# One router pass per group, gates made later, token sums on GpSimd: a float32 Strassen kernel on one core

## The chip, the cores and the metric

The kernel runs on one core of a Trainium2 chip. The metric is the time of one execution on the device in microseconds (us), lower is better. TensorE (PE in the rows) multiplies, VectorE (DVE), ScalarE (ACT) and GpSimd (POOL) work on tiles, and transfers are issued by SyncE (SP), ScalarE and GpSimd.

## The reference

`x` is 8 sequences of 256 tokens with 1024 features. Each sequence picks one of eight 1024x1024 matrices; its result goes through a base matrix and a mixture of eight low-rank adapters of rank 16 with a top-2 router.

```python
c = einsum('bsi,boi->bso', x, cond_weight[ids])          # xc below
probs = softmax(c @ W_router.T)                          # 8 experts
topk_p, topk_i = top_k(probs, 2); topk_p /= sum(topk_p)
combine = sum(one_hot(topk_i, 8) * topk_p[..., None], axis=1)
h = einsum('nd,erd->ner', c, A_stack) * combine[..., None]
lora = einsum('ner,eor->no', h, B_stack) * 2.0
out = x + c @ W_base.T + b_base + lora
```

## The kernel before

Two sequences are a pair (512 tokens), two pairs are a group; there are two groups, g = 0 and 1, and each goes through two products.

**First product.** For sequence s and output tile t (8 of 128 rows), `cond(s, t)` runs 8 wide matmuls (L827) and 8 narrow ones (L831) into one of four banks `bank_x`. ScalarE copies the low half out of the bank (L521), VectorE adds (L705) into `xp`, ScalarE rounds `xp` to the high part of `xc_hl` (L526), VectorE subtracts for the low part (L710). Every float32 operand of a product is such a pair of high and low parts: a "split" is a ScalarE cast (`hi`, L492) and then a VectorE subtraction (`lo`, L553), 128x1024 each. After each pair of sequences TensorE runs `router(p)` (L871: true float32, 32 of the 128 columns of the array for each of four token blocks, so 32 matmuls, which the trace shows as 64 records) and `lora_down(p)` (24 matmuls, the low-rank product, into bank_y1).

**Second product.** The base matrix is multiplied by a form of Strassen's scheme (Winograd's) in seven products, in the order P1, P2, P5, P6, P7, P4, P3. Each is 4 output tiles m of 12 matmuls (L812 to L814); P2, P7, P4 and P3 add 3 matmuls of `lora_up` to each tile, from the gated low-rank result `h_hl` (pair 0 of the group for P2 and P4, pair 1 for P7 and P3). Before products P5, P6, P7 and P4 stand "T" sums of tokens (two 128x1024 subtractions in `xp`), before P5, P6, P7 and P3 "S" sums of weights (two of 128x1024 in `raw`); all are on VectorE (L557), and each sum is then split. Results leave the banks by `first_pass` (L596; t1 after P1, t2 after P6) and `last_pass` (L604; C11 after P2). TensorE waits for the passes before it writes a bank again: P5 tile m for C11 m, P7 tile m for t2 m.

**Gates.** `make_gate(p)` on VectorE transposes the logits and goes through 16 small operations, each waiting for the one before, with one exponential on ScalarE. GpSimd then issues 4 small DMAs that spread the gate over rows (`gate_to_rows`, L440), VectorE multiplies (`gate_h`, L618), ScalarE rounds (`h_high`) and VectorE subtracts (`h_low`, L622). The gate of a group's first pair is made in the first product, after its second sequence; that of the second pair in the "window" between the products. GpSimd also issues the residual loads (L425) and the stores (L431). Every engine works through its own list in program order.

Of the kernel before, what the change touches and what calls it, by code (L numbers as in the profile page):

```python
# [144 lines left out]
def sum_order():  # L145
    order = [("bd", 0, 0)]
    for g in range(GROUPS):
        for kind, j in (("T", P5), ("S", P5), ("T", P6), ("S", P6), ("T", P7), ("S", P7), ("T", P4), ("S", P3)):
            order += [(kind, g, (j, 0)), (kind, g, (j, 1))]
    return order  # L150


SUM = {key: n + 1 for n, key in enumerate(sum_order())}


# [52 lines left out]
def build(nc, x, ids, w_cond, w_base, w_router, lora_a, lora_b, bias, consts, out):  # L208
    with ExitStack() as ctx:
# [27 lines left out]
        logit_sb = sb("logit_sb", [P, NQ, NR])  # L237
        logit = logit_sb[:, :, 0:EXPERTS]
# [14 lines left out]
        ps_logit, ps_h, ps_warm = bank_y[0], bank_y[1], bank_y[3]  # L253
# [12 lines left out]
        summed = sem("summed")  # L266
        cond_done = sem("cond_done")
# [4 lines left out]
        router_done = sem("router_done")  # L272
        gate_step = sem("gate_step")
# [19 lines left out]
        GATE_STEPS = 14  # L293
# [119 lines left out]
        def _(pool):  # L413
# [28 lines left out]

            for g in range(GROUPS):
# [25 lines left out]
        def _(act):  # L469
            def hi(key):  # L470
                kind, i, j = key
                if key in SUM:
                    act.wait_ge(summed, SUM[key])
                elif kind == "S":
# [6 lines left out]

                if kind == "S" and j[0] >= P5:
                    act.wait_ge(product_done, made(i, j[0] - 2, 2 * j[1] + 1))
# [14 lines left out]
            def exp_and_h(p):  # L498
                act.wait_ge(gate_step, p * GATE_STEPS + 3)
                nc.scalar.activation(expd[:], shifted[:], ACT.Exp).then_inc(exp_done, 1)  # L500
                act.wait_ge(h_done, p + 1)
                if p:
                    act.wait_ge(h_split, p)
                nc.scalar.copy(h_sb[:], ps_h[:]).then_inc(h_copied, 1)
# [10 lines left out]
            for g in range(GROUPS):  # L515
                stages = base_splits(g)
                for s in range(GSEQS * g, GSEQS * (g + 1)):
                    for t in range(KT):
# [11 lines left out]
                        if s % GSEQS == 2 and t == 2:  # L530
                            h_high(2 * g)
                    if s % GSEQS == 1:
                        exp_and_h(2 * g)

                for key in stages["window"][:2]:
                    hi(key)
                for key in stages["window"][2:]:
                    hi(key)
                exp_and_h(2 * g + 1)
                for key in stages[P1]:  # L540
                    hi(key)
                h_high(2 * g + 1)
                for j in (P2, P5, P6, P7, P4, P3):
# [4 lines left out]
        def _(dve):  # L548
# [9 lines left out]

            def t_sum(j):
                for h in range(2):  # L560
                    x11, x21 = half(xp[:, 0, 0:HT], h), half(xp[:, 0, HT:KT], h)
                    x12, x22 = half(xp[:, 1, 0:HT], h), half(xp[:, 1, HT:KT], h)
                    if j == P5:
                        total(x11, x12, x11, ALU.subtract)
                    elif j == P6:
                        total(x11, x22, x11, ALU.subtract)
                    elif j == P7:
                        total(x12, x22, x12, ALU.subtract)
                    else:
                        total(x11, x21, x11, ALU.subtract)  # L570
# [44 lines left out]
            def gate_h(p):  # L615
                dve.wait_ge(gate_in, 16 * CG * (p + 1))
                dve.wait_ge(h_copied, p + 1)
                nc.vector.tensor_tensor(h_sb[:], h_sb[:], gate_rows[:], ALU.mult).then_inc(h_gated, 1)  # L618
# [5 lines left out]

            def make_gate(p):
# [379 lines left out]
```

## Time and profile before

| | |
|---|---|
| median of 3 runs | 395.6 us (395.04 to 395.6) |
| the profiled execution, its own time | 395.35 us |
| its span in the profile | 393.6 us |
| TensorE busy | 389.0 us, 99% |
| VectorE busy | 302.3 us, 77% |
| ScalarE busy | 184.1 us, 47% |
| GpSimd busy | 49.9 us, 13% |
| granted TensorE clock | full in every slice |

The span is what the trace covers; 1.75 us of the execution's time lie around it. Busy shares are means over stages: in the second product VectorE is busy far more than 77%.

### The profile page before, as it was taken

To read this page: it belongs to the slowest core of one execution; us is meant where nothing else is said; L and a number is where in the kernel's file an instruction comes from. 1 tells how busy PE (TensorE), PEld (TensorE's weight loads), DVE (VectorE), ACT (ScalarE), POOL (GpSimd) and SP (SyncE) were. 2 spreads that over 40 slices of the span, in tenths; PEclk is the share of its full clock that TensorE was granted. 3 is DMA by queue.
4 is the path that set the end of the run, shared out by engine and by line. 5 is a ranking of instruction groups with operands and counts; after the bars stand their busy time and mean duration, and the time that the engine had idled before them with its cause. 6 is when DMAs were issued, how large, how long until landed. Compare 5 with 4: busy or idle time off the path is not lost.

```text
span 393.6 us, 5707 instructions
## 1 busy us (share of the span) xinstructions
PE 389.0 (99%) x2185; PEld 332.2 (84%) x2185; DVE 302.3 (77%) x431; ACT 184.1 (47%) x281; POOL 49.9 (13%) x84
## 2 busy tenths in 40 slices
PE   8999999999999999999999999999999999999997
PEld 7888888888888888888888888888888888888886
DVE  4797866779699999974548786778867999998322
ACT  5877734748642444332147666357656224441000
POOL 0101103110002130021130000260000202201110
PEclk9999999999999999999999999999999999999999
DMA  7998875868433146586668667499083302552222
GB/s 249 398 361 285 298 261 113 293 220 304 153 107 27 56 144 185 175 263 220 206 216 290 229 216 263 115 246 393 23 264 110 77 6 81 181 168 80 82 80 80
DMA packets 21979, 73.95 MB, mean 188 GB/s; under 512 B 3344, under 2 KB 3600, under 8 KB 21952
## 3 DMA queue, kind: packets, MB, share of 16 engines
q1 hardware_dynamic: 15984, 55.58, 41.1%
q0 software_dynamic: 5680, 16.96, 14.6%
q10 hardware_dynamic: 288, 1.05, 0.7%
q8 instruction: 17, 0.28, 0.3%
q14 instruction: 10, 0.08, 0.1%
HBM read 64.13 MB, written 8.39 MB: 184 GB/s over the span
## 4 chain that ended last, share of the span: by engine, by line
PE 98%; DMA 1%; ACT 0%; DVE 0%; ACTq 0%; issue 0%
PE bank_x L827 30%; PE bank_x L831 15%; PE bank_y L812 9%; PE bank_y L813 8%; PE bank_y L814 8%; PE bank_x L814 8%; PE bank_x L813 8%; PE bank_x L812 8%; PE bank_y L871 2%; DMA raw<-x 1%; ACT x_hl L510 0%; DVE out_sb L612 0%; ACTq L348 0%; ACT wc_hl L510 0%
## 5 line engine op out<-in xcount | busy, mean ns | idle before, releaser
L827 PE MATMUL bank_x<-x_hl,wc_hl 128*128 128x512 f32 x512 | 128.7, 393 | 0.6 <-ACT wc_hl L510 0.6
L553 DVE TENSOR_TENSOR wc_hl<-raw,wc_hl 128x1024 fp32r<-128x1024 f32 x90 | 108.5, 1221 | 18.6 <-ACT wc_hl L492 18.4
L492 ACT CAST wc_hl<-raw 128x1024 fp32r<-128x1024 f32 x90 | 93.6, 1051 | 56.3 <-DVE raw L557 22.8
L827 PEld LDWEIGHTS bank_x<-x_hl,wc_hl 128*128 128x128 f32 x512 | 92.1, 189 | 17.7 <-ACT wc_hl L510 1.3
L831 PEld LDWEIGHTS bank_x<-x_hl,wc_hl 128*128 128x128 f32 x512 | 70.0, 190 | 5.1
L831 PE MATMUL bank_x<-x_hl,wc_hl 128*128 128x256 f32 x512 | 71.5, 282 | 0.0
L521 ACT COPY xc_low<-bank_x 128x256 f32<-128x256 f32 x64 | 23.7, 370 | 35.2 <-PE bank_x L831 35.2
L705 DVE TENSOR_TENSOR xp<-bank_x,xc_low 128x256 f32<-128x256 f32 x64 | 27.0, 422 | 15.4 <-ACT xc_low L521 14.6
L812 PE MATMUL bank_x<-x_hl,wc_hl 128*128 128x512 f32 x96 | 37.3, 389 | 0.0
L813 PE MATMUL bank_x<-x_hl,wc_hl 128*128 128x512 f32 x96 | 37.3, 389 | 0.0
L814 PE MATMUL bank_x<-x_hl,wc_hl 128*128 128x512 f32 x96 | 37.3, 389 | 0.0
L596 DVE SCALAR_TENSOR_TENSOR out_sb<-bank_x,bias_sb,out_sb 128x512 f32<-128x512 f32 x32 | 23.6, 747 | 17.5 <-PE bank_x L814 15.1
L526 ACT CAST xc_hl<-xp 128x256 fp32r<-128x256 f32 x64 | 26.0, 406 | 20.7 <-DVE xp L705 20.5
L710 DVE TENSOR_TENSOR xc_hl<-xp,xc_hl 128x256 fp32r<-128x256 f32 x64 | 26.9, 421 | 7.5 <-ACT xc_hl L526 7.5
L431 POOL DMA_DIRECT2D out<-out_sb x28 | 15.4, 550 | 124.2 <-DVE out_sb L604 102.2
L425 POOL DMA_DIRECT2D out_sb<-x x32 | 22.9, 718 | 56.6 <-PE bank_x L831 56.4
L604 DVE TENSOR_TENSOR out_sb<-bank_y,out_sb 128x512 f32<-128x512 f32 x23 | 15.7, 689 | 15.1 <-PE bank_y L814 14.3
L440 POOL DMA_DIRECT2D gate_rows<-compared x16 | 9.6, 610 | 132.5 <-DVE compared L679 132.5
L492 ACT CAST x_hl<-xp 128x1024 fp32r<-128x1024 f32 x16 | 16.6, 1051 | 15.0 <-DVE xp L557 14.7
L812 PE MATMUL bank_y<-xc_hl,wc_hl 128*128 128x512 f32 x60 | 23.3, 389 | 0.0
L813 PE MATMUL bank_y<-xc_hl,wc_hl 128*128 128x512 f32 x60 | 23.3, 389 | 0.0
L814 PE MATMUL bank_y<-xc_hl,wc_hl 128*128 128x512 f32 x60 | 23.3, 389 | 0.0
(88 smaller groups left out, 504.3 us busy)
## 6 DMA issues: line engine op xcount, KB each, us to landing
raw<-w_cond SPq DMA_DIRECT2D x62, 512.0 KB, 4.7
raw<-w_base SPq DMA_DIRECT2D x24, 512.0 KB, 5.1
out_sb<-x POOLq DMA_DIRECT2D x32, 256.0 KB, 4.9
raw<-x SPq DMA_DIRECT2D x14, 512.0 KB, 5.0
out<-out_sb POOLq DMA_DIRECT2D x28, 256.0 KB, 2.4
raw<-x ACTq DMA_DIRECT2D x2, 512.0 KB, 3.8
raw<-w_cond SPq DMA_DIRECT2D x4, 256.0 KB, 3.6
gate_rows<-compared POOLq DMA_DIRECT2D x16, 64.0 KB, 3.9
```

What stands on the lines that cost most here:

```text
L492: nc.scalar.copy(split_dst(key, HI), split_src(key)).then_inc(hi_done, 1)
L521: nc.scalar.copy(xc_low[:, t % 2], bank_x[t % HT][:, TOK:]).then_inc(low_copied, 1)
L526: nc.scalar.copy(xc_hl[:, t, HI, s % 2 * TOK:(s % 2 + 1) * TOK], xp[:, s // 2 % 2, t, s % 2 * TOK:(s % 2 + 1) * TOK]).then_inc(xc_hi, 1)
L553: nc.vector.tensor_tensor(split_dst(key, LO), split_src(key), split_dst(key, HI).bitcast(F32), ALU.subtract).then_inc(lo_done, 1)
L596: nc.vector.scalar_tensor_tensor(out_sb[:, o], bank_x[m][:], bias_sb[:, i:i + 1], out_sb[:, o], ALU.add, ALU.add).then_inc(pass_done, 1)
L705: nc.vector.tensor_tensor(xc, bank_x[t % HT][:, 0:TOK], xc_low[:, t % 2], ALU.add) \
L710: nc.vector.tensor_tensor(xc_hl[:, t, LO, s % 2 * TOK:(s % 2 + 1) * TOK], xc, xc_hl[:, t, HI, s % 2 * TOK:(s % 2 + 1) * TOK].bitcast(F32), ...
L812: nc.tensor.matmul(ps, w_hi, v_hi, start=start, stop=False, skip_group_check=resumed)
L813: nc.tensor.matmul(ps, w_hi, v_lo, start=False, stop=False, skip_group_check=resumed)
L814: return nc.tensor.matmul(ps, w_lo, v_hi, start=False, stop=stop, skip_group_check=resumed)
L827: nc.tensor.matmul(ps[:], wc_hl[:, slot_of(s, t), HI, k], x_hl[:, s % 2, k].rearrange("p h n -> p (h n)"), start=(k == 0), stop=False)
L831: return nc.tensor.matmul(ps[:, TOK:], wc_hl[:, slot_of(s, t), LO, k], x_hl[:, s % 2, k, HI], start=False, stop=(k == KT - 1))
```

## The change

1. `router` runs once for a group, after its fourth sequence, with the tokens of both pairs as one moving operand: 32 matmuls of 256 columns in place of twice 32 of 128.
2. The low-rank result of the first pair stays in bank_y2 (that of the second goes to bank_y1) until `gate_h` reads it there; one copy of ScalarE falls away.
3. Both gates are made in the second product: the first at the window's start, the second after P5's first splits. Each group turns the logits of both pairs at its start.
4. The T sums go to GpSimd, four pairs of 128x1024 subtractions for a group, with a semaphore of their own, and `gate_to_rows` moves behind some of them.

```diff
             for g in range(GROUPS):
                 for c in ("t1", "t2", "t3"):
-                    if c == "t2":
-                        gate_to_rows(2 * g)
                     for m in range(HT):
...
-                gate_to_rows(2 * g + 1)
+                t_sum(g, P5)
+                gate_to_rows(2 * g)
+                t_sum(g, P6)
+                t_sum(g, P7)
                 for m in range(HT):
                     store(g, "C11", m)
...
                     residual(g, "C21", m)
+                t_sum(g, P4)
+                gate_to_rows(2 * g + 1)
...
+            def t_sum(g, j):
+                if j == P5:
+                    pool.wait_ge(router_done, g + 1)
+                pool.wait_ge(lo_done, SPLIT["T", g, ({P5: P1, P6: P5, P7: P5, P4: P6}[j], 1)])
+                for h in range(2):
...
+                    nc.gpsimd.tensor_tensor(dst, a, b, ALU.subtract).then_inc(t_summed, 1)
...
+                turn_logits(g)
+                make_gate(2 * g)
                 for key in stages["window"]:
                     lo(key)
-                make_gate(2 * g + 1)
-                t_sum(P5)
                 for key in stages[P1]:
                     lo(key)
+                gate_h(2 * g)
                 first_pass(g, "t1", 0)
+                h_low(2 * g)
...
+                        mm = nc.tensor.matmul(ps_logit[j * NR:(j + 1) * NR, 0:2 * P].rearrange("p (b n) -> p b n", b=2),
+                                              wr_sb[:, k], xp[:, :, k, j * P:(j + 1) * P],
+                                              start=(k == 0), stop=(k == KT - 1), tile_position=(0, j * NR))
...
                     if j == P2:
                         if m == 0:
                             pe.wait_ge(lo_done, SPLIT["bd", 0, 0])
+                            pe.wait_ge(h_split, 2 * g + 1)
...
+                    if s % GSEQS == GSEQS - 1:
+                        router(g)
                     if s % 2:
-                        router(s // 2)
                         lora_down(s // 2)
```

How the list of VectorE changes, from the window's end on in group 0 (before; `probs`, `compared`, `gate_pad` belong to the gate; L557 on `xp` is a T sum):

```order
L553 TENSOR_TENSOR x_hl<-xp,x_hl 128x2x512 [waits hi_done] x2
L641 STREAM_TRANSPOSE logit_sb<-bank_y 128x128 [waits router_done]
...
L679 STREAM_TRANSPOSE compared<-gate_pad 128x128 [waits gate_step]
L557 TENSOR_TENSOR xp<-xp 128x1024 x2
L553 TENSOR_TENSOR xc_hl<-xp,xc_hl 128x2x512 [waits hi_done] x2
L596 SCALAR_TENSOR_TENSOR out_sb<-bank_x,bias_sb,out_sb 128x512 [waits res_in0,product_done]
```

and the same place in the changed kernel, where L643 is `gate_h` and L648 `h_low` of the first pair:

```order
L711 STREAM_TRANSPOSE compared<-gate_pad 128x128 [waits gate_step]
L587 TENSOR_TENSOR wc_hl<-raw,wc_hl 128x1024 [waits hi_done] x2
L587 TENSOR_TENSOR x_hl<-xp,x_hl 128x2x512 [waits hi_done] x2
L587 TENSOR_TENSOR xc_hl<-xp,xc_hl 128x2x512 [waits hi_done] x2
L643 TENSOR_TENSOR h_sb<-bank_y2,gate_rows 128x512 [waits h_done,gate_in]
L617 SCALAR_TENSOR_TENSOR out_sb<-bank_x0,bias_sb,out_sb 128x512 [waits res_in0,product_done]
L648 TENSOR_TENSOR h_hl<-h_sb,h_hl 128x512 [waits h_hi]
```

The gate now comes ahead of the four window splits, the T sum is gone from the list, and the gated low-rank result is made behind the splits of P5's tokens.

GpSimd's list over group 0 in the changed kernel (L460 are the T sums, L448 the gate rows, L439 stores, L433 residual loads):

```order
L433 DMA out_sb<-x 128x2x256 [waits cond_done] x12
L460 ISA
L460 TENSOR_TENSOR xp<-xp 128x1024 [waits lo_done,router_done]
L460 TENSOR_TENSOR xp<-xp 128x1024
L448 DMA gate_rows<-compared 128x1x128 [waits gate_ready]
L448 DMA gate_rows<-compared 128x1x128 x3
L460 TENSOR_TENSOR xp<-xp 128x1024 [waits lo_done]
L460 TENSOR_TENSOR xp<-xp 128x1024
L460 TENSOR_TENSOR xp<-xp 128x1024 [waits lo_done]
L460 TENSOR_TENSOR xp<-xp 128x1024
L439 DMA out<-out_sb 128x512 [waits pass_done] x4
```

Before, this list held DMA issues alone after its first memsets; now the sums of P5 stand ahead of the first pair's gate rows, and those of P6 and P7 ahead of the stores of C11.

## Rows read from the trace of the kernel before

**Rows 1.** The page, part 1: busy time of the engines

```profile
PE 389.0 (99%) x2185; PEld 332.2 (84%) x2185; DVE 302.3 (77%) x431; ACT 184.1 (47%) x281; POOL 49.9 (13%) x84
```

**Rows 2.** Waits of TensorE (us in total, times, longest)

```profile
PE bank_y L947 <- DVE h_hl L549: 1.2, 1, 1.2
```

**Rows 3.** The chain that ended last (start us, us)

```profile
52.26 1.88 PE bank_y L871 x64
54.15 0.43 PE bank_y L812
...
59.85 1.81 PE bank_x L827 x8
...
112.11 0.23 PE bank_x L812
...
122.99 0.23 PE bank_y L812
```

**Rows 4.** Groups of TensorE by form (busy us, mean ns)

```profile
L831 PE MATMUL bank_x<-x_hl,wc_hl 128*128 128x256 f32 x512 | 71.5, 282 | 0.0
...
L812 PE MATMUL bank_y<-xc_hl,wc_hl 128*128 128x512 f32 x60 | 23.3, 389 | 0.0
...
L871 PE MATMUL bank_y<-xp,wr_sb 128*32 128x128 f32 x256 | 7.8, 274 | 0.0
```

**Rows 5.** VectorE's timeline in the window and the products P1 to P6

```profile
106.80 4.63 DVE L553 TENSOR_TENSOR wc_hl<-raw,wc_hl 128x1024 fp32r<-128x1024 f32 x4 [0.52 <-ACT wc_hl L492]
111.35 2.35 DVE L553 TENSOR_TENSOR x_hl<-xp,x_hl 128x1024 fp32r<-128x1024 f32 x2
113.62 0.31 DVE L641 STREAM_TRANSPOSE logit_sb<-bank_y 128x128 f32<-128x128 f32 x1
...
115.11 0.19 DVE L651 TENSOR_TENSOR probs<-shifted,stat 128x32 f32<-128x32 f32 x1
...
118.62 2.32 DVE L557 TENSOR_TENSOR xp<-xp 128x1024 f32<-128x1024 f32 x2
120.92 2.36 DVE L553 TENSOR_TENSOR xc_hl<-xp,xc_hl 128x1024 fp32r<-128x1024 f32 x2
...
127.45 0.68 DVE L618 TENSOR_TENSOR h_sb<-h_sb,gate_rows 128x512 f32<-128x512 f32 x1
...
132.65 1.28 DVE L604 TENSOR_TENSOR out_sb<-bank_y,out_sb 128x512 f32<-128x512 f32 x2
...
151.08 2.36 DVE L553 TENSOR_TENSOR wc_hl<-raw,wc_hl 128x1024 fp32r<-128x1024 f32 x2
153.36 0.74 DVE L596 SCALAR_TENSOR_TENSOR out_sb<-bank_x,bias_sb,out_sb 128x512 f32<-128x512 f32 x1
```

**Rows 6.** GpSimd's timeline

```profile
0.35 0.10 POOL L997 MEMSET const-uint8-127<- 128x1 uint8 x1
0.74 0.20 POOL L414 MEMSET gate_pad<- 128x128 f32 x1 [0.29 <-POOLq L997]
...
118.99 2.40 POOL L440 DMA_DIRECT2D gate_rows<-compared  x4 [19.04 <-DVE compared L679]
133.62 1.18 POOL L431 DMA_DIRECT2D out<-out_sb  x2 [12.24 <-DVE out_sb L604]
...
256.14 5.70 POOL L425 DMA_DIRECT2D out_sb<-x  x8
```

**Rows 7.** DMA issues of the whole run (KB each, us to landing)

```profile
raw<-w_cond SPq DMA_DIRECT2D x62, 512.0 KB, 4.7
...
out<-out_sb POOLq DMA_DIRECT2D x28, 256.0 KB, 2.4
...
gate_rows<-compared POOLq DMA_DIRECT2D x16, 64.0 KB, 3.9
```

**Rows 8.** DMA issues in the stretch 256 to 263 us

```profile
raw<-w_cond SPq DMA_DIRECT2D x3, 512.0 KB, 8.6
```

More of the change, by code:

```diff
@@ L142, with s_sum_order, t_sum_order @@
 SPLIT = {key: n + 1 for n, key in enumerate(split_order())}
-def sum_order():
+def s_sum_order():
     order = [("bd", 0, 0)]
     for g in range(GROUPS):
-        for kind, j in (("T", P5), ("S", P5), ("T", P6), ("S", P6), ("T", P7), ("S", P7), ("T", P4), ("S", P3)):
-            order += [(kind, g, (j, 0)), (kind, g, (j, 1))]
-    return order
-SUM = {key: n + 1 for n, key in enumerate(sum_order())}
+        for j in (P5, P6, P7, P3):
+            order += [("S", g, (j, 0)), ("S", g, (j, 1))]
+    return order
+def t_sum_order():
+    return [("T", g, (j, h)) for g in range(GROUPS) for j in (P5, P6, P7, P4) for h in range(2)]
+SUM = {key: n + 1 for n, key in enumerate(s_sum_order())}
+T_SUM = {key: n + 1 for n, key in enumerate(t_sum_order())}
 def load_order():
@@ L480, in hi @@
                     act.wait_ge(raw_in[slot], landed)
+                if kind == "T" and j[0] == P5:
+                    act.wait_ge(h_done, 2 * i + 2)
                 if kind == "S" and j[0] >= P5:
@@ L529, in _ @@
                             hi(key)
[L530 to L533, printed above, removed]
                 for key in stages["window"][:2]:
                     hi(key)
+                exp_shifted(2 * g)
                 for key in stages["window"][2:]:
                     hi(key)
-                exp_and_h(2 * g + 1)
                 for key in stages[P1]:
                     hi(key)
+                h_high(2 * g)
+                copy_h(g)
+                for j in (P2, P5):
+                    for key in stages[j]:
+                        hi(key)
+                exp_shifted(2 * g + 1)
+                for key in stages[P6][:2]:
+                    hi(key)
                 h_high(2 * g + 1)
-                for j in (P2, P5, P6, P7, P4, P3):
+                for key in stages[P6][2:]:
+                    hi(key)
+                for j in (P7, P4, P3):
                     for key in stages[j]:
@@ L557, in total @@
                 nc.vector.tensor_tensor(dst, a, b, op).then_inc(summed, 1)
[L559 to L570, printed above, removed]
             def s_sum(g, j):
@@ L616, in gate_h @@
                 dve.wait_ge(gate_in, 16 * CG * (p + 1))
-                dve.wait_ge(h_copied, p + 1)
-                nc.vector.tensor_tensor(h_sb[:], h_sb[:], gate_rows[:], ALU.mult).then_inc(h_gated, 1)
+                if p % 2:
+                    dve.wait_ge(h_copied, p // 2 + 1)
+                else:
+                    dve.wait_ge(h_done, p + 1)
+                nc.vector.tensor_tensor(h_sb[:], h_sb[:] if p % 2 else ps_h[0][:], gate_rows[:], ALU.mult) \
+                    .then_inc(h_gated, 1)
             def h_low(p):
@@ L623, in h_low, with turn_logits @@
                     .then_inc(h_split, 1)
+            def turn_logits(g):
+                dve.wait_ge(router_done, g + 1)
+                for n in range(2):
+                    nc.vector.transpose(logit_sb[:, n].rearrange("p q n -> p (q n)"), ps_logit[:, n * P:(n + 1) * P]) \
+                        .then_inc(logit_turned, 1)
             def make_gate(p):
+                logit = logit_sb[:, p % 2, :, 0:EXPERTS]
                 mx, denom, inv, two, inv2 = (stat[:, i] for i in range(5))
@@ L639, in make_gate @@
                 v4 = [P, NQ, EXPERTS, EXPERTS]
-                dve.wait_ge(router_done, p + 1)
-                chain(nc.vector.transpose(logit_sb[:].rearrange("p q n -> p (q n)"), ps_logit[:, 0:P]))
-                ready()
+                dve.wait_ge(logit_turned, p + 1)
                 chain(nc.vector.tensor_reduce(mx, logit, AX.X, ALU.max))
@@ L734, in _ @@
                 first_pass(g, "t1", 2)
-                gate_h(2 * g + 1)
                 first_pass(g, "t1", 3)
@@ L758, in _ @@
                     lo(key)
+                gate_h(2 * g + 1)
                 first_pass(g, "t2", 0)
-                t_sum(P4)
+                h_low(2 * g + 1)
                 first_pass(g, "t2", 1)
@@ L859, in cond, with router @@
                 mm.then_inc(cond_done, 1)
-            def router(p):
-                if p == 0:
+            def router(g):
+                if g == 0:
                     pe.wait_ge(wr_in, 16)
-                if p == 2:
-                    pe.wait_ge(pass_done, passed(0, "C12", HT - 1))
+                p = 2 * g + 1
                 for k in range(KT):
```

48 lines of the change are left out of this document (24 added, 24 removed).

## The prediction

> **What bounds the kernel now.** I read the page's busy times first, then TensorE's waits, then the chain that ended last, then the timelines of VectorE and GpSimd around the window. TensorE is busy for 99% of the span [rows 1], and its longest wait is 1.2 us, once, at the start [rows 2]. In the chain the matmuls follow each other without a gap: in P1, 48 of them between 112.11 and 122.99, which is 0.2267 us each [rows 3]. So only less work on TensorE can shorten the run, and any other engine can lengthen it once it is late by more than its cover. The cover is read against TensorE's schedule: P1, P5 and P6 take 10.88 us each (48 matmuls), P2 13.60 (60). In the window VectorE has almost no idle time, and most of its 128x1024 operations have both inputs in SBUF [rows 5]. GpSimd only issues transfers [rows 6].
>
> **TensorE's part.** From the router's start (52.26) to the next cond (59.85) pass 7.59 us. The 24 matmuls of `lora_down` are 24 x 0.2267 = 5.44, so one router run with its changeovers costs 2.15: 1.88 of its own and 0.27 around it, most of it in the first matmul behind it, 0.43 in place of 0.23 [rows 3]. Four runs are 8.60.
>
> What 256 columns cost no row shows. 1.88/64 is 29.4 ns from record to record, while a record lasts 274 ns [rows 4]: the four column blocks overlap. A matmul of 512 columns lasts 389 ns, one of 256 columns 282, so a column costs 0.418 ns. The router's 128 float32 columns last about as long as 256 of the others, so each record streams some 107 ns, and with four side by side 26.7 of the 29.4 ns are streaming. Doubling the columns gives 53.5 + 2.7 = 56.2 ns, times 64 = 3.59 us. Bounds: 3.42 (streaming alone) and 3.76 (twice the present). I take 3.59, since the rest looks like the price of a changeover, not of a column. A group then pays 3.59 + 0.27 = 3.86 in place of 4.30. Two groups save **0.88 us** (0.54 to 1.22). Nothing else leaves TensorE.
>
> **The new schedule, if the engines don't disturb each other.** In group 0 everything behind the first pair starts 2.15 earlier: the router at 104.52 - 2.15 = 102.37, `lora_down` at 106.23, P1 at 111.67, P2 at 122.55, P2's first `lora_up` at 125.27, P5 at 136.15, P6 at 147.0, P7 at 157.9. (104.52 is 112.11 less the 7.59 of [rows 3].)
>
> VectorE's splits begin at 104.65 (the first row of [rows 5] less 2.15); 1.14 a piece, so those of P1's weights end at 106.93. Two transposes 0.65, the rest of the gate 4.66 (5.00 from 113.62 to 118.62, less the transpose): 112.25. Window splits 4 x 1.14: 116.8. T splits of P5 2.28: 119.1. The gate rows: issued from 112.5 on for 2.4 us [rows 6], the last at 114.3, lands after 3.9 [rows 7]: 118.2, in time. `gate_h` 0.6, t1's first pass 0.66, `h_low` 0.6: 120.95, where TensorE wants it at 125.27, 4.3 us of cover. Then S sum of P5 2.3 (123.3), three passes (125.3), S splits of P5 (127.6), C11's passes as P2 yields them (the third at 133.5), T splits of P6, S sum of P6, C11's last, S splits of P6 (141.0), the second gate 4.66 (145.7), T splits, S sum and S splits of P7 (152.6), `gate_h`, t2's first pass at 153.9. P7 wants that pass at 157.9: **4.0 us of cover**. The second gate's rows stand behind the P4 sums on GpSimd and land by 152.5. Taking 8 T sums of 1.15 us off VectorE in a group therefore brings nothing, because TensorE wasn't waiting for them, and it pays for the two gates that now lie between the products. The removed copy of ScalarE is hidden too.
>
> So the sum without disturbance is 395.35 - 0.88 = 394.5 against the execution's own time, 394.7 against the median (0.25 higher), -0.22%.
>
> **The price of a T sum on GpSimd.** The trace has no arithmetic there. Its memsets take 0.10 us for 1 element and 0.20 for 128 [rows 6], 0.83 ns for an element written. A sum reads two and writes one: between 1.15 (VectorE's price, 2.32 for two [rows 5]) and 3 x 0.83 x 1024 + 0.1 = 2.65 us. I take 2.4, near the upper end, since the memset is the engine's own row. By the Trainium skill, GPSIMD Engine Reference, "Elementwise — side-by-side cycle accounting", 2048 elements take 4497 ns, which would make 2.25; no run here shows it.
>
> **The disturbance that decides.** GpSimd's sums read SBUF while VectorE works through operations with two SBUF inputs. If both need the same way in, they take turns, each holding it for a whole instruction. The rows are silent: two stores issued at 133.62 beside VectorE's work took 1.18 us [rows 6], the usual price, but an issue reads no tile. I hold turns for twice as likely as none, because VectorE takes 1.14 us for 1024 elements with two SBUF inputs [rows 5], 1.1 ns for an element of each: both inputs come in at once, and an engine that reads beside it needs a third way in. The Trainium skill, SBUF — State Buffer, "Who interferes with whom", states exactly this lock between a two-input VectorE operation and a GpSimd instruction that reads SBUF; by it the sum would be the one that follows, without it 394.7.
>
> With turns, and with GpSimd getting in where VectorE has a gap or reads a bank:
> - P5's two sums start at 107.0, under the transposes. The gate's subtraction waits until 109.4, and `probs` until 112.0, since the exponential leaves a gap for the second sum. From `probs` on the gate needs 3.5 more (115.11 to 118.62 [rows 5]): 115.6, 3.3 late.
> - T splits of P5 end at 122.4, `gate_h` 123.0. P6's first sum holds 122.4 to 124.8, `h_low` waits and ends at 125.4: **0.1 us** lost by TensorE.
> - P6's second sum comes in t1's passes (127.7 to 130.1), P7's in the passes of C11 (132.4 to 134.8, 139.4 to 141.8). S splits of P6 end at 144.1, part of the delay being absorbed in the wait for P2's third tile.
> - GpSimd stores C11 (from 141.8), loads C21 and reaches P4's sums at 147.0, in the middle of the second gate (144.1 + 4.66). Both get in between its small steps: the gate ends at 152.7 in place of 148.8.
> - T splits 155.0, S sum 157.3, S splits 159.6, `gate_h` 160.2, t2's first pass 160.85. P7 could start at 157.9: **2.9 us** lost. Its gate rows land at 158.7.
>
> That is 3.0 us for a group, 6.0 for both, since group 1 repeats the pattern. **395.35 - 0.88 + 6.0 = 400.5, against the median 400.7.** If instead GpSimd wins each tie and sends both sums of a pair ahead, `h_low` is 2.4 later and P5 and P7 lose more: some 5.8 for a group, 406.
>
> **Rivals.**
> 1. *No turns* (the other side): both engines read freely, cover 4.0 and 4.3 hold, and the time is 394.7 (394.4 to 395.1). For it: nothing in the rows shows one engine holding up the other. It decides at the 4.0 us of cover: with turns the delay at t2's pass is 6.9 us for sums of 2.4, and falls under 4.0 at about 1.7 us a sum. Cheap sums therefore end here too.
> 2. *GpSimd is simply slow.* Without turns, P5's sums stand ahead of the gate rows, from 106.2 on. Above (125.27 - 1.9 - 3.9 - 1.8 - 106.2)/2 = 5.7 us a sum the rows are late for P2. That is twice the upper bound; each further us costs 2 a group. The unpriced library row ahead of the first sum hides in the 8 us in which GpSimd waits for the router.
> 3. *Residual loads bunch up.* At the start of group 1 12 loads leave in a row. In [rows 6] 8 left in 5.70 us from 256.14, the weight loads beside them landed after 8.6 us in place of 4.7 [rows 7, 8], and TensorE did not wait [rows 2]. I expect nothing; at worst 2 us, 397.
> 4. *The router is no cheaper*: at 3.76 the saving is 0.54 and rival 1 gives 395.1, no change.
>
> **How the numbers follow.** Turns with a loss 0.63 (397 to 407, by the sum's price and by who wins ties), no turns or cheap sums 0.31, rivals 2 and 3 0.06. The predicted time is that of the likeliest, 400.7; its own range is 397.5 to 406.5. Since cases of both signs matter, the full range runs from 394.2 to 406.5. 0.2% (0.8 us) is about what a measurement of this kernel can tell from no change. Rival 1's -0.22% lies on that edge, so its 0.31 is halved: faster 0.16, same 0.16, slower 0.68.
>
> **What would show it.** Router: 64 records over 3.4 to 3.8 us, twice. GpSimd: `xp` sums of 2.2 to 2.7 us when alone. Turns: VectorE operations with two SBUF inputs (0.19 in `probs`) of 1 to 2.5 us or gaps of that size beside GpSimd sums, and waits of TensorE at P7's first tile for t2's pass or P7's splits, about 3 us in each group. The prediction is wrong if those waits are absent, or if TensorE waits at P2's `lora_up` or P5 for longer than at P7.

## The result: 415.9 us in place of 395.4

The changed kernel takes 415.87 us (414.05 to 416.31, six runs) against 395.38 of the kernel before, measured in turns on one chip: a ratio of 1.0513, 95% interval 1.0502 to 1.0524. The profiled execution took 416.31 and has a span of 414.5, 20.9 more than before. The forecast, 400.7 (394.2 to 406.5), had the sign and the mechanism, and a quarter of the size: 5.3 of 20.5 us.

The page of the changed kernel, part 1, and TensorE's waits (us in total, times, longest), to be read beside [rows 1] and [rows 2]:

```profile
PE 395.6 (95%) x2057; PEld 333.3 (80%) x2057; DVE 312.1 (75%) x415; ACT 182.2 (44%) x279; POOL 92.3 (22%) x100
```

```profile
PE bank_x L837 <- issue: 9.5, 2, 5.6
PE bank_y L837 <- DVE h_hl L648: 4.2, 2, 2.1
PE bank_y L977 <- DVE h_hl L583: 1.2, 1, 1.2
PE bank_x L852 <- ACT wc_hl L538: 1.0, 1, 1.0
```

GpSimd's 42 us more are the sums. TensorE now waits 14 us in four main places, two in a group: at P7's first tile, and at P2's first `lora_up`, for `h_low`. VectorE is busy 9.8 us longer with 16 operations fewer; those that grew are in its timeline of group 0 (start us, us; L677 the gate's subtraction, L683 `probs`, L617 the pass of a first tile, L591 an S sum):

```profile
107.41 1.78 DVE L677 TENSOR_TENSOR shifted<-logit_sb,stat 128x32 f32<-128x32 f32 x1
...
109.92 1.64 DVE L683 TENSOR_TENSOR probs<-shifted,stat 128x32 f32<-128x32 f32 x1
...
123.28 0.69 DVE L643 TENSOR_TENSOR h_sb<-bank_y,gate_rows 128x512 f32<-128x512 f32 x1 [1.54 <-DMA gate_rows<-compared]
123.88 0.74 DVE L617 SCALAR_TENSOR_TENSOR out_sb<-bank_x,bias_sb,out_sb 128x512 f32<-128x512 f32 x1
124.66 2.43 DVE L648 TENSOR_TENSOR h_hl<-h_sb,h_hl 128x512 fp32r<-128x512 f32 x1
127.01 6.73 DVE L591 TENSOR_TENSOR raw<-raw 128x1024 f32<-128x1024 f32 x2
...
148.24 5.20 DVE L683 TENSOR_TENSOR probs<-shifted,stat 128x32 f32<-128x32 f32 x1
```

and what GpSimd did in the same time:

```profile
105.95 5.55 POOL L460 TENSOR_TENSOR xp<-xp 128x1024 f32<-128x1024 f32 x2 [8.29 <-PE bank_y L896]
115.25 2.42 POOL L448 DMA_DIRECT2D gate_rows<-compared  x4 [3.75 <-DVE compared L711]
121.82 10.83 POOL L460 TENSOR_TENSOR xp<-xp 128x1024 f32<-128x1024 f32 x4 [4.15 <-DVE xc_hl L587]
...
145.75 2.86 POOL L433 DMA_DIRECT2D out_sb<-x  x4
148.62 4.75 POOL L460 TENSOR_TENSOR xp<-xp 128x1024 f32<-128x1024 f32 x2
```

Read them together. `probs` takes 0.19 us in [rows 5]; it takes 1.64 while the second of P5's sums runs, and 5.20 where both of P4's sums run, 148.62 to 153.37: it ends 0.07 us behind them. It had begun 0.38 us ahead of the first of them, while GpSimd was still issuing transfers, and group 1 repeats this. `h_low` takes 2.43 in place of 0.69. `gate_h` (0.69) and the first pass (0.74), which each read a PSUM bank, keep their usual time, though GpSimd works beside them.

TensorE pays for this twice. Its rows at the two places of group 0, each the first matmul behind the wait:

```profile
127.23 0.74 PE L837 MATMUL bank_y<-h_hl,b_hl 128*128 128x512 f32 x1 [2.10 <-DVE h_hl L648]
...
165.73 0.77 PE L837 MATMUL bank_x<-x_hl,wc_hl 128*128 128x512 f32 x1 [3.98 <-issue]
166.29 0.63 PE L838 MATMUL bank_x<-x_hl,wc_hl 128*128 128x512 f32 x1
166.72 0.63 PE L839 MATMUL bank_x<-x_hl,wc_hl 128*128 128x512 f32 x1
```

The matmuls behind 165.73 start 0.43 us apart and not 0.227: the clock is at its lower level, 1.2 GHz in place of 2.4. The stretches (us; busy time of PE, PEld, DVE, ACT, POOL; granted clock; DMA share; GB/s) show it:

```profile
128.00:132.00 4.00, 4.00 (x13) 3.13 (x13) 4.00 (x2) 1.05 (x1) 4.00 (x2) 0.67 0.01 4
132.00:136.00 4.00, 4.00 (x20) 3.29 (x19) 4.00 (x5) 2.23 (x3) 0.65 (x1) 1.00 0.00 0
...
164.00:168.00 4.00, 2.27 (x6) 1.82 (x6) 3.70 (x5) 3.00 (x4) 0.00 (x0) 0.60 0.85 253
168.00:172.00 4.00, 4.00 (x12) 3.14 (x11) 4.00 (x6) 1.41 (x2) 0.00 (x0) 0.55 0.37 149
```

**The ledger.** From P1's start to the next group's first matmul are 87.04 us before and 98.05 now (111.37 to 209.42): +11.0. The distances between the starts of matmuls split it; a wait counted so is some 0.16 us longer than in the list of waits, which counts from the end of a matmul's record. P2 and its `lora_up` (122.25 to 139.82) take 17.57 in place of 13.60: 2.26 of waiting and 1.71 of lower clock. At P7's first tile TensorE waits 4.14, and 2.9 go to the clock behind it. Group 1 has the same +11.0 up to its last tile: waits of 2.27 at P2, 0.5 at P5 and 5.7 at P7, and 2.4 of clock. That is 14.9 of waits and 7.0 of clock in all, less 0.83 saved at the two routers and 0.2 at the run's start: 20.9. This is the profiled execution, the slowest of the six; its mean clock was 0.979, that of the others 0.983 to 0.984.

### The profile page after: what moved, and what is told of

It reads as the page before. It is cut to its first block, busy times and chain, and to the rows that moved or that the text cites. A ratio compares the mean times of both kernels' runs of the same rounds, so it can differ in the third digit from the quotient of the medians.

```text
span 414.5 us, 5460 instructions
## 1 busy us (share of the span) xinstructions
PE 395.6 (95%) x2057; PEld 333.3 (80%) x2057; DVE 312.1 (75%) x415; ACT 182.2 (44%) x279; POOL 92.3 (22%) x100
## 4 chain that ended last, share of the span: by engine, by line
PE 67%; DVE 22%; DMA 4%; issue 4%; ACT 2%; POOL 1%; ACTq 0%; DVEq 0%
PE bank_x L852 29%; PE bank_x L856 15%; DVE raw L591 5%; PE bank_x L837 5%; PE bank_x L838 5%; PE bank_x L839 5%; DVE wc_hl L587 4%; DVE probs L683 3%; PE bank_y L837 3%; PE bank_y L838 3%; PE bank_y L839 3%; DMA gate_rows<-compared 3%; DVE x_hl L587 2%; DVE out_sb L625 1%; DMA raw<-x 1%
## 5 line engine op out<-in xcount | busy, mean ns | idle before, releaser
L852 PE MATMUL bank_x<-x_hl,wc_hl 128*128 128x512 f32 x512 | 128.6, 392 | 1.0 <-ACT wc_hl L538 1.0
L852 PEld LDWEIGHTS bank_x<-x_hl,wc_hl 128*128 128x128 f32 x512 | 92.1, 189 | 18.0 <-ACT wc_hl L538 1.5
L856 PEld LDWEIGHTS bank_x<-x_hl,wc_hl 128*128 128x128 f32 x512 | 70.0, 190 | 5.1
L460 POOL TENSOR_TENSOR xp<-xp 128x1024 f32<-128x1024 f32 x16 | 42.3, 2673 | 105.1 <-PE bank_y L896 96.8
L837 PE MATMUL bank_x<-x_hl,wc_hl 128*128 128x512 f32 x96 | 39.6, 412 | 9.5 <-issue 9.5
L838 PE MATMUL bank_x<-x_hl,wc_hl 128*128 128x512 f32 x96 | 39.1, 408 | 0.0
L839 PE MATMUL bank_x<-x_hl,wc_hl 128*128 128x512 f32 x96 | 39.0, 407 | 0.0
L433 POOL DMA_DIRECT2D out_sb<-x x32 | 22.8, 717 | 71.2 <-PE bank_x L856 71.2
L439 POOL DMA_DIRECT2D out<-out_sb x28 | 15.4, 550 | 100.5 <-DVE out_sb L625 78.7
L617 DVE SCALAR_TENSOR_TENSOR out_sb<-bank_x,bias_sb,out_sb 128x512 f32<-128x512 f32 x32 | 23.4, 745 | 17.8 <-PE bank_x L839 15.1
L837 PEld LDWEIGHTS bank_x<-x_hl,wc_hl 128*128 128x128 f32 x96 | 19.1, 199 | 14.3 <-issue 10.3
L591 DVE TENSOR_TENSOR raw<-raw 128x1024 f32<-128x1024 f32 (+1 forms) x17 | 28.3, 1699 | 0.0
L837 PE MATMUL bank_y<-xc_hl,wc_hl 128*128 128x512 f32 x60 | 23.4, 390 | 0.3 <-issue 0.3
L838 PE MATMUL bank_y<-xc_hl,wc_hl 128*128 128x512 f32 x60 | 23.4, 389 | 0.0
```

What stands on the lines that cost most here:

```text
L460: nc.gpsimd.tensor_tensor(dst, a, b, ALU.subtract).then_inc(t_summed, 1)
L591: nc.vector.tensor_tensor(dst, a, b, op).then_inc(summed, 1)
L837: nc.tensor.matmul(ps, w_hi, v_hi, start=start, stop=False, skip_group_check=resumed)
L838: nc.tensor.matmul(ps, w_hi, v_lo, start=False, stop=False, skip_group_check=resumed)
L839: return nc.tensor.matmul(ps, w_lo, v_hi, start=False, stop=stop, skip_group_check=resumed)
L852: nc.tensor.matmul(ps[:], wc_hl[:, slot_of(s, t), HI, k], x_hl[:, s % 2, k].rearrange("p h n -> p (h n)"), start=(k == 0), stop=False)
```

## The experiments

Two theories at the start. A (turns): a GpSimd sum and a VectorE operation with two SBUF inputs exclude one another, so sums lengthen VectorE's list. B (reorder): the loss comes from the new place of the gates, and the sums only happen to lie there. Each run is one edit, beside the kernel before on the same chip.

**1. The changed kernel with its T sums back on VectorE.**

```diff
-                t_sum(g, P5)
                 gate_to_rows(2 * g)
-                t_sum(g, P6)
-                t_sum(g, P7)
...
+                t_sum(P5)
...
                 last_pass(g, "C11", 1)
+                t_sum(P6)
...
+                t_sum(P7)
                 make_gate(2 * g + 1)
...
                 h_low(2 * g + 1)
+                t_sum(P4)
```

> The changed kernel, with the eight T sums of a group back on VectorE: P5's behind the window splits, P6's after C11's second pass, P7's ahead of the second gate, P4's behind the second h_low. One router for a group and both gates in the second product stay. Theory A (GpSimd's sums and VectorE's two-input operations take turns, and that is the whole loss): VectorE's list, priced with the rows of before, reaches h_low of the first pair at 123.3 (wanted 125.3) and t2's first pass at 156.6 (wanted 157.9), so TensorE never waits and only the router's saving is left: 394.5 us, 0.2% under before. Theory B (the two gates between the products overload VectorE, wherever the sums stand): VectorE has 9.2 us more of its own work for a group than in the changed kernel, TensorE waits at P7 for several us, the time stays above 402 us.

Measured: 395.66 us, 1.0009 [1.0000, 1.0018]. The whole 5% hangs on the engine of the sums; the other three edits cost nothing that stands out. Theory A's 394.5 was 1.2 us too low. Part of that has a place, in group 1:

```profile
347.70 0.69 DVE L635 TENSOR_TENSOR h_sb<-h_sb,gate_rows 128x512 f32<-128x512 f32 x1 [0.83 <-DMA gate_rows<-compared]
348.31 0.74 DVE L609 SCALAR_TENSOR_TENSOR out_sb<-bank_x,bias_sb,out_sb 128x512 f32<-128x512 f32 x1
```

The pass that frees P7's bank stands behind `gate_h`, which stands behind the second gate's rows; P6 and P7's first tile take 13.83 in place of 13.60. With smaller losses beside it that is 0.5 us in the profiled execution, which at 395.15 was the fastest of twelve; where the others lose more was not traced.

**2. The kernel before with only its T sums on GpSimd.** All else stays: two routers, the gates in their old places.

> The kernel before with nothing changed but the T sums, which go to GpSimd as in the change (P5's ahead of the second pair's gate rows, P6's and P7's behind them, P4's behind C21's loads). Theory A: the sums hold up VectorE as in the changed kernel, but h_low is not wanted before P7, so no loss at P2. VectorE loses 6.9 us of sums of its own up to t2's first pass and is held for 3 us in the gate, up to 9 us by the sums of P6 and P7 and 2 to 5 us by those of P4: 7 to 10 us more against a cover of 4.4 us at P7. TensorE waits 1 to 5 us at P7 in each group and its clock falls behind the wait: 398 to 410 us. Theory B: the gates stay where they were, VectorE is relieved, 395.4 us.

Measured: 415.53 us, 1.0513 [1.0498, 1.0529]. With run 1, theory B falls. But the expectation is missed too: the time lies above its 398 to 410, and TensorE waits not at P7 but at P5. That it equals the time of the whole change is chance, since the waits are others. The S sums of P5 show why:

```profile
PE bank_y L820 <- issue: 15.3, 2, 7.7
```

```profile
123.27 2.41 POOL L448 DMA_DIRECT2D gate_rows<-compared  x4 [10.92 <-DVE compared L691]
125.68 9.46 POOL L460 TENSOR_TENSOR xp<-xp 128x1024 f32<-128x1024 f32 x4
```

```profile
125.79 11.57 DVE L582 TENSOR_TENSOR raw<-raw 128x1024 f32<-128x1024 f32 x2
```

The four sums run through at their bare price, 9.46 for four, and the first S sum, issued 0.1 us behind them, stands for all of it. It is 9.2 us late. Here VectorE lost the tie four times running.

P4's sums of the same run, also directly behind GpSimd's own issues, show the reverse:

```profile
154.51 8.71 POOL L460 TENSOR_TENSOR xp<-xp 128x1024 f32<-128x1024 f32 x2
```

```profile
152.99 2.36 DVE L578 TENSOR_TENSOR x_hl<-xp,x_hl 128x1024 fp32r<-128x1024 f32 x2
155.27 2.36 DVE L582 TENSOR_TENSOR raw<-raw 128x1024 f32<-128x1024 f32 x2
157.61 6.70 DVE L578 TENSOR_TENSOR wc_hl<-raw,wc_hl 128x1024 fp32r<-128x1024 f32 x2
```

Three VectorE operations (the second of the first row and both of the next) run at their old length and GpSimd's first sum stands for them: it lasts 5.38 us. Only then do the two engines alternate. Group 1 does the same.

**3. GpSimd as busy, but only writing.** Each T sum becomes 13 memsets of 128x128, each behind the end of the one ahead; the T sums are left out of the computation.

```diff
-                    nc.gpsimd.tensor_tensor(dst, a, b, ALU.subtract).then_inc(t_summed, 1)
+                    for _ in range(12):
+                        if idle[0]:
+                            pool.wait_ge(idle_done, idle[0])
+                        nc.gpsimd.memset(idle_sb[:], 0.0).then_inc(idle_done, 1)
+                        idle[0] += 1
+                    pool.wait_ge(idle_done, idle[0])
+                    nc.gpsimd.memset(idle_sb[:], 0.0).then_inc(t_summed, 1)
```

> The changed kernel with each T sum on GpSimd replaced by 13 memsets of a tile of 128x128 of its own, one waiting for the other: GpSimd is busy for 2.5 to 4 us in place of each sum and writes SBUF, but reads nothing. The T sums are left out of the computation; the splits behind them run on unsummed tokens. Theory A in its narrow form (only GpSimd's reads stand in the way of a second SBUF input of VectorE): VectorE's operations keep their times (0.19 us for probs, 1.21 for an S sum), TensorE does not wait, 394.5 us; up to 400 if the memsets are so slow that the gate rows come late. In its wide form (any GpSimd operation on SBUF holds the pair): VectorE's operations stretch as in the changed kernel, above 405 us. Theory B: above 402 us as well, with no operation stretched.

Measured: 399.58 us, 1.0093 [1.0066, 1.0120]. GpSimd is held 3.3 us for each sum, more than by a sum, and VectorE's operations have their old lengths:

```profile
106.79 3.08 POOL L466 MEMSET idle_sb<- 128x128 f32 x12 [8.26 <-PE bank_y L906]
```

```profile
109.19 0.19 DVE L693 TENSOR_TENSOR probs<-shifted,stat 128x32 f32<-128x32 f32 x1
...
158.56 0.69 DVE L653 TENSOR_TENSOR h_sb<-h_sb,gate_rows 128x512 f32<-128x512 f32 x1 [5.44 <-DMA gate_rows<-compared]
```

Nor is any other two-input operation of VectorE in the whole trace longer than its form was in run 1 by more than 0.01 us. So it isn't GpSimd's work as such that stretches VectorE: the sums do it, which read SBUF, and the memsets, which only write, do not. The 0.9% that stays is another thing: the second gate, done at 146.3, has its rows queued behind the longer memsets; they are issued at 150.18, and `gate_h` waits 5.44 for them.

**4. Each sum in four pieces** of 128x256, the same bytes and the same places.

```diff
-                    nc.gpsimd.tensor_tensor(dst, a, b, ALU.subtract).then_inc(t_summed, 1)
+                    for k in range(2):
+                        for c in range(2):
+                            cut = (slice(None), k, slice(c * TOK, (c + 1) * TOK))
+                            op = nc.gpsimd.tensor_tensor(dst[cut], a[cut], b[cut], ALU.subtract)
+                    op.then_inc(t_summed, 1)
```

> The changed kernel with each T sum of 128x1024 cut into four instructions of 128x256. Theory A with turns taken for one instruction: a VectorE operation waits for one piece of 0.65 us at most, so probs falls from 5.2 us to under 1, h_low from 2.43 to about 1.3; the S sums of P5 still alternate, but with pieces. The wait at P2 (2.26 us) nearly goes, that at P7 (4.2 us) is halved: 400 to 406 us. If GpSimd keeps the way in for its whole run of sums and VectorE gets none of the gaps: nothing gained, 416 us or more, since each piece has its own start.

Measured: 404.99 us, 1.0261 [1.0237, 1.0286]: half the loss goes.

```profile
108.66 0.62 DVE L687 TENSOR_TENSOR probs<-shifted,stat 128x32 f32<-128x32 f32 x1
...
124.30 1.17 DVE L652 TENSOR_TENSOR h_hl<-h_sb,h_hl 128x512 fp32r<-128x512 f32 x1
125.39 3.43 DVE L595 TENSOR_TENSOR raw<-raw 128x1024 f32<-128x1024 f32 x2
```

These operations now wait about half a microsecond each, and TensorE 0.3 us in each group at P2's `lora_up`, 3.1 and 3.7 at P7. Its waits behind the sums come to 7.5 us in place of 14.9, and in the profiled execution, the fastest of four at 402.54, the clock stayed full. Here a turn is held for one instruction, and its price follows the length of the neighbour's instruction.

**5. Filler matmuls in TensorE's waits.** With weights of zero, 8 of 512 columns ahead of P2's wait and 16 at P7's start, to price the lower clock by itself.

```diff
+                if j == P7:
+                    for _ in range(16):
+                        nc.tensor.matmul(bank_y[3][:], zeros[:], h_hl[:, 0, HI], start=False, stop=True,
+                                         skip_group_check=True)
...
+                            for _ in range(8):
+                                nc.tensor.matmul(bank_y[3][:], zeros[:], v[:, 0, HI], start=True, stop=True)
                             pe.wait_ge(h_split, 2 * g + 1)
```

> The changed kernel with idle matmuls on TensorE where it waits: 8 of 512 columns with zero weights ahead of the wait for the first h_low in P2 (1.8 us of the 2.3 us wait), 16 at the start of P7 (3.6 us of 4.2 to 5.6 us), adding zeros to a bank. Nothing else waits differently. Theory C (the wait itself costs 6.4 us in group 0, and the half clock that follows it in the profile another 1.7 us at P2 and 2.9 us at P7): the clock stays at full speed and 4 to 5 us fall away in each group: 406 to 409 us, with P2's and P7's matmuls at 0.227 us each behind the wait. Rival: the slow stretch behind the waits has another cause than TensorE's idleness: 416 us.

Measured: 411.42 us, 1.0421 [1.0398, 1.0445]. The same stretches as above now read

```profile
128.00:132.00 4.00, 4.00 (x20) 3.33 (x19) 4.00 (x2) 1.05 (x1) 4.00 (x2) 1.00 0.00 0
...
168.00:172.00 4.00, 4.00 (x19) 3.34 (x18) 4.00 (x6) 1.53 (x2) 0.00 (x0) 1.00 0.37 152
```

with 20 and 19 matmuls for 13 and 12. 4.4 us come back, of the 7.0 that the ledger puts down to the clock; 4 to 5 in each group were expected, so the time misses 406 to 409. Of the rest 1.5 us are eaten in group 0: full speed behind P2 brings TensorE earlier to a VectorE that is late anyway, so that P5 waits 0.56 us, where it had not waited, and P7's first tile comes 5.11 after its turn in place of 4.14.

**6. The better order.** From run 1: the second gate ahead of P7's T sum, its exponential earlier on ScalarE (not printed), and t2's first pass ahead of `gate_h`.

```diff
-                t_sum(P7)
                 make_gate(2 * g + 1)
+                t_sum(P7)
...
-                gate_h(2 * g + 1)
                 first_pass(g, "t2", 0)
+                gate_h(2 * g + 1)
                 h_low(2 * g + 1)
```

> The kernel with the sums back on VectorE (the first of the experiments), with the second gate ahead of P7's T sums, its exponential ahead of the casts of P7's tokens on ScalarE, and t2's first pass ahead of the second gate_h. There TensorE waited up to 0.4 us at P7 for t2's first pass, which stood behind gate rows that landed 0.8 us late. Theory D (that wait ate the router's saving, which the traces put at 0.31 us a group): no wait at P7, 0.6 us under before: 394.85 us, ratio 0.9984. Rival (the router's saving is given back elsewhere, in each execution): 395.5 us, no change.

Measured: 394.57 us, 0.9985 [0.9975, 0.9996], the fastest of all. TensorE's only wait is that of the start; P1 to the next group takes 87.04, to the hundredth what it took before. What is gained is the router's alone, 0.83 us by the traces and 0.86 by the medians. t2's pass is done 2 us before P7 (157.41) wants it:

```profile
154.60 0.74 DVE L612 SCALAR_TENSOR_TENSOR out_sb<-bank_x,bias_sb,out_sb 128x512 f32<-128x512 f32 x1
```

**7. The sums on GpSimd, out of the way.** Those of P6 and P7 start only once `h_low` is done, and the second gate's rows go ahead of P4's sums.

```diff
                 gate_to_rows(2 * g)
+                pool.wait_ge(h_split, 2 * g + 1)
                 t_sum(g, P6)
...
-                t_sum(g, P4)
                 gate_to_rows(2 * g + 1)
+                t_sum(g, P4)
```

> The changed kernel with GpSimd's sums of P6 and P7 held until h_low of the first pair is done, and P4's behind the second pair's gate rows. h_low and probs are then free of them. If turns are always one for one: the wait at P2 falls from 2.3 to 0.5 us and P7 gains the 5 us of probs, 397 to 401 us. If a run of GpSimd sums that begins together with a VectorE operation keeps it out until the run ends, as at P5's S sums in the kernel where the sums alone were moved (11.6 us for two): now the first S sum of P5 starts together with the run of four, VectorE stands for 9 us, and the time is 410 to 417 us.

Measured: 412.40 us, 1.0426 [1.0400, 1.0451]. P2's wait shrinks to 0.8 us, the second gate runs undisturbed (`probs` 0.19), and the wait at P7 stays (5.1 and 4.3 us), because the turns move to P7's own S sums. Group 0:

```profile
154.88 7.54 DVE L592 TENSOR_TENSOR raw<-raw 128x1024 f32<-128x1024 f32 x2
```

```profile
153.02 2.40 POOL L448 DMA_DIRECT2D gate_rows<-compared  x4 [3.51 <-DVE compared L712]
155.42 4.77 POOL L460 TENSOR_TENSOR xp<-xp 128x1024 f32<-128x1024 f32 x2
```

Again two sums at their bare price (4.77), directly behind the issue of transfers, and VectorE stands for both, though its S sum had begun 0.54 us ahead of the first. Group 1 has the same order of work and goes the other way, one for one:

```profile
354.94 4.56 DVE L592 TENSOR_TENSOR raw<-raw 128x1024 f32<-128x1024 f32 x2
```

```profile
355.60 6.15 POOL L460 TENSOR_TENSOR xp<-xp 128x1024 f32<-128x1024 f32 x2
```

In the first pair's region, where the sums start behind a semaphore wait, the two engines alternate too.

**8 to 10. Who wins the tie?** Theory E: where the sums follow GpSimd's own DMA issues without a wait, it keeps its turn over the whole run of sums. P4's sums of run 2 and group 1 of run 7, above, already speak against it as a rule. Run 8 puts a memset of 128x16 behind each sum of run 2, with no wait. Run 9 puts one memset and a wait for its end between run 2's gate-row issues and P6's sums. Run 10 does the same in the changed kernel, ahead of P4's sums. The edit of run 9:

```diff
+                nc.gpsimd.memset(idle_sb[:, g], 0.0).then_inc(idle_done, 1)
+                pool.wait_ge(idle_done, g + 1)
                 t_sum(g, P6)
```

> The kernel before with only the T sums on GpSimd, and behind each sum a memset of 128x16 to a tile of its own, which reads nothing (0.1 us). If VectorE lost the way in because GpSimd's sums follow each other without a gap: the two S sums of P5 take 6 to 8 us in place of 11.6, TensorE's wait at P5 falls from 7.7 to 3 or 4 us: 402 to 408 us. If who comes next doesn't depend on a gap: 415.5 us as without the memsets.

> The kernel before with only the T sums on GpSimd, and a memset of 128x16 with a wait for its end between the first DMA issues of the gate rows and P6's sums. In three places so far VectorE stood through a whole run of GpSimd sums (P5's S sums 11.6 us, probs 5.2 us, P7's S sums 6.4 us for the first), and each time the first sum came directly behind GpSimd's own DMA issues; behind a wait the two engines took turns. Theory E (it is the place directly behind DMA issues that lets the run through): P5's two S sums fall from 11.6 to 6.7 us or less, TensorE's wait at P5 from 7.7 to about 3 us: 402 to 408 us. Rival (it is the moment alone, or chance): 11.6 us stay, 415.5 us.

> The changed kernel with the same pause between GpSimd's loads of C21 and P4's sums. Theory E: probs of the second gate waits for one sum and not for two, 2.6 us in place of 5.2, or one of the later steps takes the second turn; P7 then starts 1 to 2.5 us earlier in each group: 410 to 414 us. Rival: probs stays at 5.2 us, 415.9 us.

Measured: run 8 415.83 us, 1.0524 [1.0506, 1.0543], the S sums 11.69 long. The memsets made no gap: the second sum starts at 127.88, where the first ends at 127.90. So run 8 shows only that an instruction between the sums changes nothing. Run 9 408.24 us, 1.0334 [1.0316, 1.0351], at the edge of theory E's 402 to 408, with TensorE's wait at P5 4.2 us in place of 7.7. VectorE and GpSimd of run 9:

```profile
125.53 4.55 DVE L586 TENSOR_TENSOR raw<-raw 128x1024 f32<-128x1024 f32 x2
...
131.32 1.56 DVE L634 TENSOR_TENSOR h_sb<-h_sb,gate_rows 128x512 f32<-128x512 f32 x1
...
134.53 5.02 DVE L582 TENSOR_TENSOR wc_hl<-raw,wc_hl 128x1024 fp32r<-128x1024 f32 x2 [0.98 <-ACT wc_hl L521]
```

```profile
125.38 0.15 POOL L477 MEMSET idle_sb<- 128x16 f32 x1
125.62 12.84 POOL L462 TENSOR_TENSOR xp<-xp 128x1024 f32<-128x1024 f32 x4
```

The four sums that took 9.46 now take 12.84: GpSimd waits as well. VectorE's operations grow by 2.2, 0.9 and 2.7, where one had grown by 9.2. Run 10 takes 410.53 us, 1.0386 [1.0346, 1.0425]:

```profile
149.93 0.19 DVE L687 TENSOR_TENSOR probs<-shifted,stat 128x32 f32<-128x32 f32 x1
...
150.95 2.50 DVE L698 TENSOR_TENSOR compared<-compared,const_sb 128x256 f32<-128x256 f32 x1
153.48 2.50 DVE L700 TENSOR_TENSOR compared<-compared 128x256 f32<-128x256 f32 x1
```

Here `probs` takes 0.19, though it lies beside the last of GpSimd's issues just as it did without the pause, where it stood for 5.20: so an issue of transfers alone does not hold VectorE up. The 5.0 us on `probs` became 2.1 on each of two comparisons, one sum each. TensorE's waits at P7 fall from 9.5 to 5.9 us over both groups; the rest of the 5.3 us that the run gained goes with the clock, whose mean is 0.992 in its profile and 0.979 without the pause. Runs 8 to 10 show that a pause with a wait changes who gets in. That the place behind DMA issues is the cause isn't shown: run 2's P4 and run 7's group 1 have it too and went the other way, and the pause also changes who comes first. In run 9 the S sum begins 0.09 us ahead of the first sum (125.53, 125.62), in run 2 0.11 behind it (125.79, 125.68). Who comes first isn't the whole answer either, since `probs` of the changed kernel came 0.38 ahead and lost.

**11. Two narrow routers in a row**, at the place of the wide one in run 6: two passes of 128 columns in place of one of 256.

```diff
-                for k in range(KT):
+                for b in range(2):
+                    for k in range(KT):
...
-                                              wr_sb[:, k], xp[:, :, k, j * P:(j + 1) * P],
+                                                  wr_sb[:, k], xp[:, b, k, j * P:(j + 1) * P],
```

> The fastest kernel so far (sums on VectorE, second gate first) with the router's 256 columns cut again into two passes of 32 matmuls of 128 columns, one behind the other at the same place. It splits the 0.31 us that a group gains. If the columns that stream together are worth 0.17 us, the router takes 2 x 1.88 = 3.76 us here in place of 3.59, and the rest of the gain, 0.14 us, is the changeover that falls away. If wide matmuls bring nothing, it takes 3.59 us here too.

Measured, one run: 395.9 us. The time says nothing of the router, since 2.4 us of waits for the first weights lie at this run's start, where run 6 has none in its list. First the wide router of run 6, then the two in a row; behind each, `lora_down` starts at 105.56 and 107.25:

```profile
101.97 3.66 PE L895 MATMUL bank_y<-xp,wr_sb 128*32 128x256 f32 x64
```

```profile
103.62 3.70 PE L896 MATMUL bank_y<-xp,wr_sb 128*32 128x128 f32 x128
```

From first record to `lora_down` it is 3.59 and 3.63. One wide operand is worth 0.04 us against two in a row; two routers apart cost 2 x 1.88 = 3.76. The gain, 0.41 us a group by the traces and not the 0.31 of the expectation, is nearly all in not coming twice.

## Why the prediction was right and where it was wrong

**What bounds the kernel: right.** TensorE sets the time, and each loss sits where it waits. Run 6 closes it: no wait, 0.15% faster.

**The router: right in its price and its gain.** The 64 records take 3.59 us as forecast. From the start of group 1 to its P1, two routers with all around them, TensorE took 104.51 us before (198.98 to 303.49) and takes 104.09 now (209.42 to 313.51): 0.41 a group and 0.83 in all, against 0.88 forecast. The changeover of a router measures 0.23 us: `lora_down` takes 5.61 behind a router and 5.47 without, and a `cond` ahead of a router 44.76 where it takes 44.67 ahead of `lora_down`. The 0.27 of the forecast is near it partly by luck. Its 7.59 runs to a row of the chain [rows 3] that starts where the matmul before ends; between starts of matmuls, 52.19 and 59.69, it is 7.50, and what lies ahead of the router was not in it.

**A sum on GpSimd: right.** The 16 last from 2.37 to 3.39 us, median 2.41 (forecast 2.4); the long ones contain a wait for VectorE. The figure that the forecast named from the Trainium skill, GPSIMD Engine Reference, "Elementwise — side-by-side cycle accounting", made it 2.25 as an estimate; the trace is 7% above that.

**Turns: right as a mechanism.** Runs 2 and 3 show it from both sides: the sums alone cost 5%, and GpSimd work without reads stretches nothing. The Trainium skill, SBUF — State Buffer, "Who interferes with whom", has this lock, and rows agree with it also in what it leaves alone: operations that read a bank keep 0.69 and 0.74. In the window the forecast even hit the times: the subtraction done at 109.2 (109.4 forecast), `probs` at 111.6 (112.0), the gate at 114.9 (115.6).

**The steps that failed** are those on which the size rests.
- "`h_low` waits and ends at 125.4: 0.1 us lost". It ended at 127.1. The last gate rows landed at 123.25, since they took 6.2 us where 3.9 was taken; the same rows take up to 6.5 in run 1, so it isn't the sums that slow them. Then `h_low`, ready at 124.66, met a sum that had begun at 124.16 and stood for 1.7 us. TensorE lost 2.26 us.
- "P6's second sum comes in t1's passes" and P7's "in the passes of C11". This is the assumption under the whole sum, that GpSimd gets in only where VectorE has a gap or reads a bank. It takes every second turn, or all: the S sums of P5 took 6.73 in place of 2.35, and in run 2 11.57.
- "Both get in between its small steps: the gate ends at 152.7". Both of P4's sums ran first, and `probs` waited 5.0 us; the gate ended at 156.8, t2's first pass started at 164.88 in place of 160.2. TensorE lost 4.14 and 5.7 us at P7 where 2.9 was forecast. In group 0 VectorE's lateness was 4.0 us larger than this wait shows, since P2 and its `lora_up` had held TensorE itself up by as much (17.57 in place of 13.60).
- The clock had no term at all. [rows 2] has no wait above 1.2 us, so nothing in the trace before spoke of it, yet the sum forecast waits of 2.9 us twice and took full speed behind them. It cost 7.0 us by the ledger; run 5 got 4.4 back.

14.9 us of waits stand for 6.0 forecast. The remark on GpSimd winning each tie, "406", named the right danger; even it, with the clock left out, ended at the top of the range and 10 us short.

**The rivals.** *No turns* is out by runs 2 and 3. *Residual loads*: no wait lies at group 1's start. *The router no cheaper*: its gain is small but there, as run 6 shows. The forecast that waits at P2 or P5 "for longer than at P7" would make it wrong came true only in run 2 and in runs 8 and 9, which build on it; in the changed kernel it is 4.5 us at P2 and 9.9 at P7.

**Open:** who gets the next turn. GpSimd kept it over a whole run of sums in three places (P6's and P7's sums of run 2, P4's of the changed kernel, P4's in group 0 of run 7), each time directly behind its own DMA issues. But VectorE kept it over three operations in P4's place of run 2, behind such issues too, group 1 of run 7 alternates there, and so do the pieces of run 4. Behind a wait the engines alternated wherever VectorE had two-input work. What decides it was not found, and the size of the loss hangs on it.

## What to carry to other kernels

Moving elementwise work off a VectorE that nothing waited for bought nothing here, and putting it on GpSimd made VectorE pay for it again: for each sum that reads SBUF, count one VectorE operation with two SBUF inputs late by up to the sum's full length, and as the worst case all sums of a row at once (5 to 9 us here). If such work must go to GpSimd, cut it small (a quarter of the size halved the loss), try a wait ahead of it (worth 7.3 us in run 9 and 5.3 in run 10), and keep it away from the short operations on which a gate or a split hangs. And where a change brings waits to a TensorE that had none, allow for slower matmuls behind them: here 7.0 us behind 14.9 of waits, though not behind each.

## What was not expected of the hardware

- Who wins a tie follows no rule that the traces show: the same pair of engines alternates one for one (6.73 us for two S sums beside two sums), lets GpSimd run four through (11.57 for two), or lets VectorE run three through (5.38 for one sum on GpSimd). A 0.15 us memset with a wait for its end ahead of the sums changes it (12.84 against 9.46 us for the four sums); memsets between them, without a wait, don't.
- A VectorE operation of 128x32 elements, 0.19 us of work, lasted 5.20 us, and in its record it had begun 0.38 us ahead of the first sum that it stood for.
- Equal waits cost unequally. Behind group 0's wait of 2.26 us at P2 the granted clock fell (0.67 from 128 to 132, above); behind group 1's of 2.27, at 329.38, it did not, as the same view shows:

```profile
328.00:332.00 4.00, 2.62 (x12) 2.20 (x13) 4.00 (x2) 0.59 (x1) 4.00 (x3) 1.00 0.00 0
```

- Gate rows of 64 KB landed 3.7 to 6.5 us after their issue, where it was 3.6 to 4.7 before. In their new place two 512 KB loads of SP are under way beside the first pair's (issued at 116.09 and 117.22), where none was beside the rows at 118.99 before. That the transfers delay each other is the likely reason; no run moved one of them alone.
